# One core, four fused layers: K stores and an ordering copy moved, unread matmuls added on TensorE

## The reference, cut to what matters

```
x = x + mask * (irfft(rfft(x*mask, 2L) * rfft(K, 2L))[:L] + D * x)   # long convolution, one K of 1024 taps per channel
x = x + (x @ B1[id1].T) @ A1[id1].T      # adapter, rank 16, 8 of them
x = x + (x @ B2[id2].T) @ A2[id2].T      # adapter, rank 16, 64 of them
x = x + einsum('bct,bcd->bdt', x, w[id3]) + b[id3]   # 64 x 64 channel mix
```

## Time and profile before

| | |
|---|---|
| median of 3 runs | 784.6 us (781.02 to 784.93) |
| the profiled execution | 789.68 us, span 787.9 us |
| PE busy | 714.3 us, 91% of the span |
| DVE, ACT, POOL busy | 576.3, 435.5, 385.2 us |
| mean granted TensorE clock | 0.958 of full |
| DMA | 219.96 MB, 279 GB/s mean |

### The profile page before, as it was taken

How to read it: one execution, slowest core, us unless ns; L and a number is a source line. 1 busy time by engine, 2 the same in 40 slices (tenths; PEclk the granted TensorE clock), 3 DMA queues, 4 the chain that set the end, 5 groups by cost and what they waited for, 6 DMA issues and landing times.

```text
span 787.9 us, 19729 instructions
## 1 busy us (share of the span) xinstructions
PE 714.3 (91%) x6624; PEld 541.5 (69%) x6624; DVE 576.3 (73%) x1116; ACT 435.5 (55%) x760; POOL 385.2 (49%) x680
## 2 busy tenths in 40 slices
PE   2299998979979969999989999499999999999997
PEld 2277776758858847777767777377767777777774
DVE  7677985675856837686766866278888888888885
ACT  5535535545524643553635433157777777777775
POOL 1000188888881000005677700267677676766672
PEclk9599999989989999999999999779999999999999
DMA  6487899788897896989889895579999999999974
GB/s 217 119 283 249 277 303 325 254 306 280 259 345 241 279 318 210 333 253 314 278 297 276 261 349 191 225 244 320 310 300 322 314 310 310 321 317 315 315 269 158
DMA packets 122231, 219.96 MB, mean 279 GB/s; under 512 B 20738, under 2 KB 80706, under 8 KB 122178
## 3 DMA queue, kind: packets, MB, share of 16 engines
q1 hardware_dynamic: 103026, 166.56, 66.3%
q10 hardware_dynamic: 9936, 33.59, 10.9%
q0 software_dynamic: 9216, 19.15, 7.8%
HBM read 146.35 MB, written 72.91 MB: 278 GB/s over the span
## 4 chain that ended last, share of the span: by engine, by line
PE 60%; DMA 17%; SPq 5%; issue 4%; DVE 4%; ACT 3%; POOL 1%; POOLq 1%; ACTq 0%; DVEq 0%
PE ps L1064 23%; PE ps L1385 10%; DMA outt<-in_L_cond_A 9%; PE ps L1372 7%; PE ps L1418 5%; DMA x_rows<-xt 5%; PE ps L187 4%; PE ps L1401 3%; PE ps L1400 3%; SPq L344 2%; DMA d_rows<-khl 2%; PE ps L1391 2%; PE ps L1430 1%; ACT xTh L194 1%; DMA diff<-d_rows 1%
## 5 line engine op out<-in xcount | busy, mean ns | idle before, releaser
L1064 PE MATMUL ps<-toep,xTh 128*128 128x512 f16 (+3 forms) x1024 | 214.4, 305 | 2.5 <-DMA diff<-d_rows 2.2
L1064 PE MATMUL ps<-toep,xTl 128*128 128x512 f16 (+3 forms) x512 | 149.3, 304 | 0.0
L1064 PEld LDWEIGHTS ps<-toep,xTh 128*128 128x128 f16 x1024 | 99.3, 100 | 56.1 <-issue 4.3
L811 POOL DMA_INDIRECT gnow<-g_rows,idx_g x64 | 59.6, 931 | 145.1 <-DMA g_rows<-g_out 118.9
L787 POOL DMA_INDIRECT wnow<-in_L_cond_weights,idx_w x64 | 62.4, 976 | 102.3 <-DVEq L1001 85.3
L1255 POOL DMA_INDIRECT asel<-a_rows,idx_a x64 | 71.8, 1121 | 75.7 <-PE ps L1401 74.1
L1250 POOL COPY bsel<-bt 128x256 f16 x256 | 93.2, 407 | 4.1 <-issue 3.8
L1030 DVE TENSOR_TENSOR ps<-ps,common 128x512 f32<-128x512 f32 x64 | 44.6, 696 | 65.3 <-ACT common L853 65.1
L1340 DVE TENSOR_TENSOR xTl<-ps,xTh 128x1024 f16<-128x1024 f32 x64 | 78.4, 1224 | 12.5 <-ACT xTh L1299 9.2
L1064 PE MATMUL ps<-diff,xTh 128*128 128x256 f16 x512 | 87.3, 273 | 0.0
L853 ACT ACTIVATE common<-ps 128x256 f32<-128x256 f32 x64 | 24.3, 379 | 109.1 <-PE ps L1064 109.1
(11 more groups left out here) (227 smaller groups left out, 1750.0 us busy)
## 6 DMA issues: line engine op xcount, KB each, us to landing
toep<-k_rows SPq DMA_DIRECT2D x64, 384.0 KB, 6.9
diff<-d_rows SPq DMA_DIRECT2D x64, 384.0 KB, 8.5
xt<-in_x SPq DMA_DIRECT2D x32, 512.0 KB, 4.7
x_rows<-xt ACTq DMA_DIRECT2D x32, 512.0 KB, 5.5
xt<-x_rows SPq DMA_DIRECT2D x32, 512.0 KB, 7.2
out_dram<-outt SPq DMA_DIRECT2D x32, 512.0 KB
out_dram<-diff SPq DMA_DIRECT2D x32, 512.0 KB
toep<-x_rows SPq DMA_DIRECT2D x24, 512.0 KB, 6.6
```

What stands on the lines that cost most here:

```text
L811: gp.indirect_dma_start(m.gnow[:, v, :], None, m.g_rows, bass.IndirectOffsetOnAxis(ap=m.idx_g[0:64, q:q + 1], axis=0)).then_inc(g_gathered ...
L1064: last = PE.matmul(out, xs[x_part], rhs(part), start=start and k == 0, stop=stop and k == 2)
```

## The change

The two float16 parts of K lie side by side in the tile `khl` now, so that each half and row table is one DMA: `store_k` issues 4 DMAs where it issued 8, and 64 is waited for in place of 128. SP no longer waits for K at u == 5: it issues the stores, skips that turn's Toeplitz load, goes on to `load_x`, and at u == 6 waits for K and issues two Toeplitz loads, the one left over (h + 2) and the regular one (h + 3). On ACT the ordering copy stands at u % 4 == 1, between `high_sum` and `copy_common`, where it stood at u % 4 == 0 behind `store_x1`. `k_decay` dv moved from u == 5 to u == 6. PE gets three runs of matmuls that nobody reads (`keep_busy`): 33 at the end of setup into bank 7, 16 at the end of the channel stage and 12 at the start of the pair stage into bank 2.

```
+WARM = (33, 16, 12)
...
-    m.khl = sb("khl", [P, 2, KP, TC], F16)
+    m.khl = sb("khl", [P, KP, 2, TC], F16)
...
+def keep_busy(nc, out, w, x, count):
+
+    for n in range(count):
+        nc.tensor.matmul(out, w, x, start=True, stop=True)
...
     for e in halves:
         for n, rows in enumerate((m.k_rows, m.d_rows)):
-            for part in range(2):
-                dst = rows[bass.ds(k * E + e * KP, KP), part, 0:L].rearrange("q (a c) -> a q c", c=TC)
-                sp.dma_start(dst, m.khl[64 * e + 32 * n:64 * e + 32 * n + 32, part, :, :]).then_inc(m.k_stored, 16)
+            dst = rows.rearrange("h s t -> (h s) t")[bass.ds(2 * (k * E + e * KP), 2 * KP), 0:L].rearrange("m (a c) -> a m c", c=TC)
+            src = m.khl[64 * e + 32 * n:64 * e + 32 * n + 32, :, :, :].rearrange("a q s c -> a (q s) c")
+            sp.dma_start(dst, src).then_inc(m.k_stored, 16)
...
                 k_products(nc, m, pe, 0, 6)
+
+                pe.wait_ge(m.par01_ready, 1)
+                pe.wait_ge(m.xTh_ready, 1)
+                keep_busy(nc, ps[:, 7, :], m.xTh[:, 0, 0, :], m.xTh[:, 0, 0:4, :].rearrange("p j n -> p (j n)"), WARM[0])
...
                             if make_k and u == XU - 3:
                                 store_k(m, sp, i + 1)
-
-                                sp.wait_ge(m.k_stored, 128 * (i + 2))
+                            if make_k and u == XU - 2:
+
+                                sp.wait_ge(m.k_stored, 64 * (i + 2))
+                                load_toeplitz(m, sp, h + 2, (u + 2) % U)
...
-                            load_toeplitz(m, sp, h + 3, (u + 3) % U)
+                            if not (make_k and u == XU - 3):
+                                load_toeplitz(m, sp, h + 3, (u + 3) % U)
...
-                        if start_k and u == 5:
+                        if start_k and u == 6:
                             act.wait_ge(m.tables_ready, i + 2)
                             k_decay(nc, m, i + 2, m.dv, 0, m.decay_v_ready)
...
+                        if group and u % U == 1:
+
+                            act.wait_ge(a_loaded, 16 * g)
+                            S.activation(by_k.rearrange("p (k a r) -> p k a r", k=J, a=8),
+                                         nat_a.rearrange("p (a k r) -> p k a r", a=8, k=J), ACT.Copy).then_inc(a_ordered, 1)
                         if not (first and u == 0):
                             copy_common(h - 1, first and u < 2)
                         if not (first and u < 2):
                             store_x1(h - 2, (u - 2) % XU)
-                        if group and u % U == 0:
-
-                            act.wait_ge(a_loaded, 16 * g)
-                            S.activation(by_k.rearrange("p (k a r) -> p k a r", k=J, a=8),
-                                         nat_a.rearrange("p (a k r) -> p k a r", a=8, k=J), ACT.Copy).then_inc(a_ordered, 1)
...
                 turns(pe, body)
+                pe.wait_ge(g_out_ready, G)
+                keep_busy(nc, ps[:, 2, :], m.xTh[:, 1, 0, :], m.xTh[:, 1, 0:4, :].rearrange("p j n -> p (j n)"), WARM[1])
...
+                keep_busy(nc, ps[:, 2, :], m.iwh[:, 0, :], m.iwh[:, 0:4, :].rearrange("p q n -> p (q n)"), WARM[2])
                 turn(0, 0, 16)
                 turns(pe, body)
```

More of the change, by code:

```diff
@@ L324, in k_high @@
         rows = slice(64 * e, 64 * e + 64)
-        nc.scalar.activation(m.khl[rows, 0, :, :], k_bank(m, bank)[rows, :, e * TC:e * TC + TC], ACT.Copy).then_inc(m.k_high, 1)
+        nc.scalar.activation(m.khl[rows, :, 0, :], k_bank(m, bank)[rows, :, e * TC:e * TC + TC], ACT.Copy).then_inc(m.k_high, 1)
 def k_low(nc, m, dve, k, bank):
@@ L332, in k_low @@
         rows = slice(64 * e, 64 * e + 64)
-        nc.vector.tensor_tensor(m.khl[rows, 1, :, :], k_bank(m, bank)[rows, :, e * TC:e * TC + TC], m.khl[rows, 0, :, :],
+        nc.vector.tensor_tensor(m.khl[rows, :, 1, :], k_bank(m, bank)[rows, :, e * TC:e * TC + TC], m.khl[rows, :, 0, :],
                                 ALU.subtract).then_inc(m.khl_ready, 1)
@@ L448, in _ @@
                 store_k(m, sp, 0, (0,))
-                sp.wait_ge(m.k_stored, 128)
+                sp.wait_ge(m.k_stored, 64)
                 sp.wait_ge(pad_stored, 16)
@@ L869, in body @@
                         if make_k and u == 4:
-                            act.wait_ge(m.k_stored, 128 * (i + 1))
+                            act.wait_ge(m.k_stored, 64 * (i + 1))
                             k_high(nc, m, act, i + 1, 3)
-                        if start_k and u == 5:
+                        if start_k and u == 6:
                             act.wait_ge(m.tables_ready, i + 2)
```

## The result

The changed kernel takes 757.79 us (median of 4 runs, 755.92 to 761.17) against 783.05 (4 runs, 781.02 to 784.93) for the kernel before beside it: a ratio of 0.9683, 95% interval 0.9632 to 0.9734. Its profiled execution took 756.05 us, span 754.2, where before it was 789.68 and 787.9.

The account below looks back on a forecast made before the run. It took PE, stalled in turns 1 to 4 by 23.15 us of waits and 6.9 us of half speed, as the bound; 22.6 + 1.9 + 0.8 + 1.0 = 26.3 us off the median 784.6 gave 758.3 us, range 747 to 775.

Parts of the forecast that it names:

- likeliest case: Whole kernel: all terms hold and 26.3 us go, giving 758 us; chance 0.64 for 748 to 766.
- Ordering copy: Turns 1 to 4: a late A holds `common`, no longer the operand copies; 22.6 us gained, between 8 and 30.
- first example: Turn 1, plain half: PE needed xSl at 125.4, but it came at 127.5, behind ACT's copy of A.
- 2 us a turn: Waits that stay in halves with K stores: 1 us for Toeplitz, another at ACT's next `high_x`; 7 us over 3.5 turns.
- the 5.1 us: Profiled execution before, 789.68 us, lay this far above the median 784.6; the same sum was taken from the median.
- K stores: Channel 48: Toeplitz load, tied to the store of channel 44, goes out earlier; 1.9 us gained, between 0 and 3.
- `k_decay`: ACT at u == 6: the same 3 us one channel later, where ACT would wait for the convolution; no effect.
- 33 matmuls: End of setup: unread matmuls end just covered at 35.2, first transposes run faster; 0.8 us gained, bounds +4.6 and -1.8.
- 16 and 12 matmuls: Between the stages: the 12 run at 2.4 GHz and speed the first transposes; 1.0 us gained, from -2.3 to +3.2.
- bad bound: Start of the pair stage: the 12 matmuls at 1.2 GHz take 5.2 us, to 510.4; the term becomes -2.3 us.
- Late A: Turns 1 to 4: A's time counts from its burst's first Toeplitz load, so A comes at 156.4; 772 us, chance 0.20.
- Slower by Toeplitz loads: Seven chunk boundaries: first Toeplitz load stands behind a load of x; diff landing in 15 us gives 816 us; chance 0.05.

Follow-up runs that it names:

- e1: The kernel before with only the ordering copy moved, to u % 4 == 1 ahead of `common`: 759.21 us, ratio 0.9694.
- e5: The kernel before, copy in its old place, with B and A loaded one channel earlier: 760.43 us, ratio 0.9713.
- e2: The kernel before with only four K stores and SP's wait at u == 6; copy and `k_decay` in old places: 782.75 us, ratio 0.9974.
- e3: The changed kernel without the unread matmuls, all three counts zero: 758.69 us, ratio 0.9667.
- f2: The e4 kernel without any unread matmuls: 760.17 us, ratio 0.9664.
- f1: The e4 kernel unchanged, run again: 756.83 us, ratio 0.9653.
- f4: The e4 kernel with the old layout of `khl` and eight K stores: 757.75 us, ratio 0.9647.
- e4: The changed kernel with SP waiting for K at u == 5 again, Toeplitz load ahead of the load of x: 753.17 us, ratio 0.9612.
- e6: The e4 kernel with B and A loaded one channel later, at u % 4 == 3: 779.94 us, ratio 0.9956.
- e8: The e4 kernel with B and A loaded one channel earlier, at u % 4 == 1: 754.69 us, ratio 0.9625.
- e7: The e4 kernel with only the 33 unread matmuls in setup kept: 757.93 us, ratio 0.9662.

## Why the prediction was right, step by step

The median, 757.79, is the predicted 758; the likeliest case came true, and its main mechanism is shown from both sides (e1 by the copy's place, e5 by A's time, e2 by leaving both). The terms are less good than their sum.

**Ordering copy.** Predicted 22.6 us, 30.1 of loss less 7.5 that stay. The prediction's first example is read slightly wrong: at 125.4 PE stood in `turn_b` for khl, and the long waits for xSl (4.94, 4.66 and 5.41 us) lie in the halves with K stores. The root is the same, since DVE makes khl behind xSl. Before:

```profile
128.67 1.97 PE L1111 MATMUL ps<-ident,bsel 128*128 128x128 f32 x8 [3.29 <-DVE khl L333]
163.90 1.97 PE L187 MATMUL ps<-ident,xt 128*128 128x128 f32 x8 [4.94 <-DVE xSl L213]
```

A's time was right, 154 to 155 forecast for the second place and 154.92 measured, but by two errors that offset each other: A was issued at 144.76, not near 142.5, and took 10.2 us, not 11.8. The step that failed is "2 us a turn": the 1 us of Toeplitz wait came once, as 0.4, and the microsecond that a late `common` was to cost at the next `high_x` did not come, nor did it in e1. 1.5 us of waits stay, and 0.9 of them, at 146.87, come before the late copy. The two profiles differ by 31.1 us from channel 8 to 40, against 22.6; with the copy alone (e1) it is 27.9.

That the median still fits is partly luck. The profiled execution of before seems to have held more stall than a usual one: e2, with the copy in the same old place, took 249.5 us from channel 8 to 40 in its profile for 256.9, at a median close to that of before. A residual too large by 6 was set off by a loss too large by 5 to 7, the 5.1 us that the prediction took off as a shift of the whole profile. That this excess lay in the stalls is argued from two profiles, not shown.

**K stores.** Predicted 1.9 us at channel 48, from a Toeplitz load tied to the store of channel 44. The tie is there; the step that failed is the landing times. The store landed 7.4 us after its issue (353.19 to 360.58), not 6.2, and diff came 7.1 us after its own (361.91 to 369.06), where before it came 5.8 after (394.69 to 400.51), so PE's wait grew by 0.9 us. In the kernels with the wait at u == 6 (after, e2, e3) it was 2.3 to 3.0 us, none shorter than before, and in those with it at u == 5 it was 1.5 to 2.7. The term also left out the lower clock behind this wait, since the prediction saw none after waits under 3.3 us; it is there after 2.18 us before and 3.03 in the change, and it is not there after 2.94 in e3. With it the stretch from channel 47 to 48 varies too much to compare, 8.1 to 10.5 us with the wait at u == 6 and 7.3 to 10.1 with it at u == 5. Alone (e2) the stores gave -2.0 us in the median, interval -4.6 to +0.4. In the time the sign of this term stays open; it is small.

**`k_decay`.** No wait of PE answers to it, and it had no run of its own: e1, with it in the old place, is equal to the change.

**33 matmuls.** Predicted 0.8 us; 1.2 between the two profiles, and 2.0 and 2.2 where nothing else differs (e3 and f2 against after and f1, to channel 8). Their end was forecast well: 35.2, and 34.3 (the change) to 35.4 (f4) in the eight profiles that have them. The size of the gain was too small. Part of it hangs on the kernel compared with: without the 33, the second transposes came at 43.45 to 43.83 in the three kernels with eight stores (before, e1, e5) and at 44.63 to 44.87 in the three with four (e2, e3, f2), where the granted clock from 40 to 41 us was still 0.50; in the other three it was 1.00 there. Why is not shown. In the medians the 33 are too little to see.

**16 and 12 matmuls.** Predicted 1.0 us. The step that failed is that the 12 "should run at 2.4 GHz": in the change, e4 and f4 they took 4.44 us, near the 5.2 of the bad bound, and the transposes came 2.3 us later; in f1, e6 and e8 they took 2.75. Even there the first transposes began 8.4 us after channel 63's end, 0.6 later than before, and ended only 0.3 earlier. The end of the run does not show it, as the pair stage varies by more.

**Rivals.** Late A's premise came true in e1, where A was there at 156.59, and its price did not; in the change A came at 154.92, ahead of the rival's 156.4. Its rule, from the Trainium skill, "DMA: Bandwidth & Descriptors", section "Queues, rings and completion order", agrees with three profiles: from its own issue A took 10.2 us in the change and 10.5 in e1 (146.09 to 156.59), and 7.5 in e5 (144.49 to 152.01), where a load of x and a second Toeplitz pair no longer stood ahead of it in the burst. From the burst's first Toeplitz load it took 14.8 us in the change, 14.3 in e1 and 9.3 in e5, for the 16.9 that the rival carried over, so neither count gives a fixed time. Slower by Toeplitz loads: diff landed in 7.6 us, not 12.5. DMA issues of the changed kernel, 100 to 330 us (answers to the earlier trace rows):

```profile
diff<-d_rows SPq DMA_DIRECT2D x33, 384.0 KB, 7.6
x_rows<-xt ACTq DMA_DIRECT2D x17, 512.0 KB, 5.7
```

No version is surely better than the change: those with the copy moved, SP's wait at u == 5 and B and A in time (e4, e7, e8, f1 to f4) have ratios of 0.9612 to 0.9664, all under its 0.9683, with intervals that reach into its own. That waiting at u == 6 helps is shown by no run.

## What to carry to other kernels

When an engine's copy waits for a DMA, ask what stands behind it in that engine's order: here 31.3 us of such waits on an engine that is 55% busy cost some 25 us, and moving one instruction behind the copies that the next stage needs, or loading its data one channel earlier, took all of it away within the noise. Charge a late instruction only for what a reader downstream will miss, with its slack counted out; `common` was 2.3 us late in the change and 3.6 in e1, and PE did not wait for it. A sum made against a profiled execution that is longer than its median should ask which of its stalls makes it so.

## What the runs showed of the hardware

Matmuls issued to hold the clock across a gap of 2.4 us did not do so reliably: the same 12, after the same gap, ran down to 0.50 in three profiles (4.44 us: the change, e4, f4) and stayed at 1.00 in three (2.75: e6, e8, f1). The Trainium skill, "TensorE: Matmul & The Clock Gate", Part 1, says that the number of matmuls at the lower clock varies from run to run of one kernel. It says so of the start; here it is the fall that varies, and e4 and f1, which are one kernel, differ in it.

A wait of 2 to 3 us had the lower clock behind it in some profiles and not in others: at channel 48 PE ran at 0.62 after 2.18 us (before) and at 0.56 after 3.03 us (the change), and stayed at 1.00 after 2.42 us in f4 and 2.94 us in e3.
